# Zero rows under the 33-row halves of the node products of a two-network graph kernel

## The chip, the cores and the metric

The kernel runs on one core of a Trainium2 chip. The metric is the device time of one execution in microseconds (us), as the median of the runs. A core has a tensor engine (PE in the profile; its weight loads are listed apart as PEld), a vector engine (DVE), a scalar engine (ACT), GpSimd (POOL), which here issues the gathers, and SyncE (SP), which issues most other transfers.

## The reference, cut to what matters

There are 3125 nodes with 128 features and 100000 edges. Two message-passing rounds on 160 features per node come first, then three attention rounds on 128 features. A round of the first network is this, with D = 160:

```python
ecat = jnp.concatenate([h[src], h[dst]], axis=-1)
em = jax.nn.relu(_layernorm(ecat @ wm.T + bm, gm, bem)) * w[:, None]
msum = jax.ops.segment_sum(em, dst, num_segments=n)
messages = msum / (cnt + 1e-08) * valid
tw = jax.nn.sigmoid(h @ wg.T + bg)
h_new = jax.nn.relu(_layernorm(jnp.concatenate([h, messages], axis=-1) @ wu.T + bu, gu, beu))
return tw * h_new + (1 - tw) * h
```

After the two rounds the result is multiplied by `w_out`, each row is normalised and added to the input, and the attention rounds start from that. The node products, `h @ wm.T` (in two halves, one for the source and one for the target of an edge), the two halves of the product with `wu.T`, and `h @ w_out.T`, have 160 rows to sum over. The array of PE takes 128, so each is made of two matmuls that add up in PSUM: one over features 0 to 127, and one over features 128 to 159 with a row of ones for the bias, 33 rows of data.

## The kernel before

**Tiling.** Nodes stand in 28 blocks of 112 rows, edges in 812 tiles of 128, sorted by target. A round has a node part and an edge part. In the edge part (the loop around lines 1203, 1224 and 1227) POOL gathers one row of a node table per edge, one indirect transfer per tile (line 557), at most 32 tiles ahead of PE. PE adds the target's part with a one-hot matmul (line 1224) to the gathered rows (line 1227), ACT and DVE normalise, and PE sums the messages by target with a second one-hot matmul (line 1203), which DVE adds to the accumulator (line 1792).

**The node part between two edge parts.** All of it is in four quarters of seven blocks. `updated(q)` on PE turns seven blocks of summed messages (two transposes each, lines 1236 and 1237), ACT copies them from PSUM to `MT1` and `MT2` (lines 931 and 932), and PE multiplies them with `WU1` (line 1248, 128 rows) and `WU2` (line 1249, 33 rows). DVE's `update(q)` takes the seven results out of PSUM (line 1620), normalises them with a square root made by ACT (line 854) and ends with the quarter's new features (line 1640, milestone `h{l}_{q}`). `products(q)` on PE waits for that milestone, turns the seven new blocks (lines 1126 and 1128, copies by ACT at lines 846 and 848 to `HT1` and `HT2`) and multiplies them with `WPQ1` (line 1266, 128 rows) and `WPQ2` (line 1267, 33 rows); ACT copies the results out (line 964). The program order of PE is `updated(0)`, `updated(1)`, `products(0)`, `updated(2)`, `products(1)`, `updated(3)`, `products(2)`, `products(3)`. ACT makes the roots of quarter q+1 in the middle of `products(q)`, behind its fourth block's copies.

**After the quarters.** At the end of round 0 the table goes to memory and POOL may begin the gathers of round 1. PE goes on with the target's half of the next round's product, 28 more blocks (`taq1`, lines 1171 and 1172, taken out by DVE at line 1666), and only then starts the edge part of round 1. At the end of round 1 the product with `w_out` takes the place of the table, DVE also normalises the rows (`rows_out`), and the attention rounds follow. At the very start, `tab0` and `taq0` (the same lines 1171 and 1172, 56 blocks) stand beside POOL's scatter of the sorted edges (line 542). In both edge parts, 28 blocks are also multiplied with the first half of `WU1` and `WU2` inside the loop (lines 1210 and 1211).

**Where things stand.** Everything lies in one big array `AR` of which `carve(n, parts)` gives out n columns; it moves on by n columns whatever number of partitions is asked. `HT2`, `MT2`, `WPQ2` and `WU2` are carved with 33 partitions, so the 95 partitions below them are never written by that name. Each engine's order is that of its program; a semaphore is awaited where the code says.

Of the kernel before, what the change touches and what calls it, by code (L numbers as in the profile page):

```python
# [14 lines left out]
B = 112  # L15
# [45 lines left out]
D = 160  # L61
# [51 lines left out]
def gnn_program(nc, a, out):  # L113
    with ExitStack() as ctx:
# [41 lines left out]
        STE = carve(4 * 1024).rearrange("p (g n) -> p g n", g=4)  # L156
        sort_end = cur[0]
        HT1 = carve(3 * B).rearrange("p (g n) -> p g n", g=3)
        HT2 = carve(3 * B, 33).rearrange("p (g n) -> p g n", g=3)
        MT1 = carve(3 * B).rearrange("p (g n) -> p g n", g=3)  # L160
        MT2 = carve(3 * B, 33).rearrange("p (g n) -> p g n", g=3)

        gB = carve(D)
        nbeB = carve(D)
# [2 lines left out]
        guB = carve(D, B)  # L167
        beuB = carve(D, B)
        WPQ1 = carve(2 * D)
        WPQ2 = carve(2 * D, 33)  # L170
        BLb = carve(GW, B)
        BRb = carve(GW, B)
        BPQ = BLb[0:1, :]
        WU1 = carve(2 * 161)
        WU2 = carve(2 * 161, 33)
        BU = carve(161, 1)
        attB = gB[:, 0:GW]
        att2B = nbeB[:, 0:128]
# [115 lines left out]
        WP2v = WPQ2.rearrange("p (k f) -> p k f", k=2)  # L294
        WU1v = WU1.rearrange("p (k f) -> p k f", k=2)
        WU2v = WU2.rearrange("p (k f) -> p k f", k=2)
        XJ1 = XJ.rearrange("p (g f) -> p g f", f=D)
        HZ = AR[:, NB * 128:NB * 128 + 16 * 4 * GW]

# [743 lines left out]
        def tensor_program(e):  # L1043
# [110 lines left out]
            for l in range(2):  # L1154
                for p, c0 in ((f"tab{l}", 0), (f"taq{l}", D))[l:]:

                    for b in range(-1, NB):
                        if b + 1 < NB:
                            w.wait_ge(s_dve, DV["henc"] if l == 0 else DV["h0_3"])
                            turn_block(p, b + 1, H, (b + 1) % 2, True)  # L1160
                        if b < 0:
                            continue
                        o = PS[2 + b % 4][0:B, 0:D]
                        w.wait_ge(s_ts, tp_at(p, b))
                        w.wait_ge(s_dve, DV[f"w{l}"])
                        if p == "tab0":
                            w.wait_ge(s_aev, aev_at(p, b - 4))
                        else:
                            w.wait_ge(s_aev, aev_at(f"tab{l}", NB - 1))
                            w.wait_ge(s_dev, dev_at(p, b - 4))  # L1170
                        e.matmul(o, HT1[:, b % 3, :], WPQ1[:, c0:c0 + D], start=True, stop=False)
                        done(e.matmul(o, HT2[:, b % 3, :], WPQ2[:, c0:c0 + D], start=False, stop=True), s_mm)

                w.wait_ge(s_dve, DV[f"wf{l}"])
                w.wait_ge(s_dev, dev_at(f"taq{l}", NB - 1))
# [4 lines left out]
                for j in range(-2, NQ + 2):  # L1180
# [14 lines left out]
                    for u in (2 * j, 2 * j + 1):  # L1195
                        v_ = u - 4
                        if 0 <= v_:

                            w.wait_ge(s_vt, pair_at(l, v_))
                            w.wait_ge(s_sw, quad_at(l, v_ // 2))  # L1200
                            w.wait_ge(s_acc, pair_at(l, v_ - 2) if v_ >= 2 else 0)
                            for t in (2 * v_, 2 * v_ + 1):
                                x = e.matmul(PS[4 + v_ % 2][0:B, (t % 2) * 161:(t % 2 + 1) * 161], SW[:, (t // 4) % 4, t % 4, :],  # L1203
                                             VB[:, v_ % 6, t % 2, :], start=True, stop=True, skip_group_check=True)
                            b = OWN[l].get(v_ // 2 - 1) if v_ % 2 == 0 else None
                            if b is not None:

                                o = PS[4][0:B, 322:483]
                                w.wait_ge(s_tsu, own_at(l, b))
                                e.matmul(o, HT1[:, b % 3, :], WU1v[:, 0, :], start=True, stop=False, skip_group_check=True)  # L1210
                                x = e.matmul(o, HT2[:, b % 3, :], WU2v[:, 0, :], start=False, stop=True, skip_group_check=True)
                            done(x, s_scat)
                        if 0 <= u < 2 * NQ:
                            if l == 0:
# [24 lines left out]
                def updated(q, bank):  # L1239
                    for k in range(-1, CH):  # L1240
                        b = q * CH + k
                        if k + 1 < CH:
                            sums_turned(b + 1)
                        if k < 0:
                            continue
                        o = PS[bank + BANK[k]][0:B, PLACE[k] * 161:(PLACE[k] + 1) * 161]
                        w.wait_ge(s_tsu, upd_at(l, b))
                        e.matmul(o, MT1[:, b % 3, :], WU1v[:, 1, :], start=True, stop=False, skip_group_check=True)
                        done(e.matmul(o, MT2[:, b % 3, :], WU2v[:, 1, :], start=False, stop=True, skip_group_check=True), s_mmu)

                def products(q, bank):
                    p, n = ("tab1", D) if l == 0 else ("out", 128)
                    w.wait_ge(s_dve, DV[f"h{l}_{q}"])
                    for k in range(-1, CH):
# [9 lines left out]
                        else:  # L1264
                            w.wait_ge(s_w[5], 48)
                        e.matmul(o, HT1[:, b % 3, :], WPQ1[:, 0:n], start=True, stop=False, skip_group_check=True)
                        done(e.matmul(o, HT2[:, b % 3, :], WPQ2[:, 0:n], start=False, stop=True, skip_group_check=True), s_mm)


                p = "tab1" if l == 0 else "out"  # L1270
# [112 lines left out]
        def vector_program(e):  # L1383
# [6 lines left out]
            def mile(inst, name):  # L1390
                _, n = w.done(inst, s_dve)
                assert n == DV[name], (n, name)
# [148 lines left out]
            for i in range(2):  # L1541
                x = e.tensor_copy(BT[:, i * (T // 2):(i + 1) * (T // 2)], PS[6 + i][0:1, 0:T // 2])
            mile(x, "bt")
            mile(e.memset(HT2[32:33, :, :], 1.0), "ht1")

            w.wait_own()
# [547 lines left out]
```

## Time and profile before

| | |
|---|---|
| median of 3 runs | 7023.26 us (7016.12 to 7036.81) |
| profiled execution, its own time | 7019.37 us |
| its span on the core | 7017.6 us |
| PE, PEld, DVE, ACT, POOL busy | 77%, 65%, 63%, 36%, 66% |
| chain that ended last, by engine | PE 17%, POOL 16%, DVE 15%, issue 10%, DMA 4% |
| costliest groups | gathers of the attention rounds (line 565) 2304.1 us, gathers of the two first rounds (line 557) 1543.6 us |

The page gives shares of the whole span. The stages have different limits, so it is read together with the views by time: the busy times and the granted clock of PE in a stretch, the engines' instructions in order of time, and the chain of waits. Times in those views count from the start of the span. One float32 matmul shows as two records of the same line ("x2"), and a transpose as one; ends of matmuls are modelled, so the spacing of starts is what is measured.

### The profile page before, as it was taken

Reading aid. Unit: us, or ns where it says so; the run is one execution under the profiler, and the core shown is the slowest. Engines: PE = TensorE matmul, PEld = TensorE weight load, DVE = VectorE, ACT = ScalarE, POOL = GpSimd, SP = SyncE. Lnnn points to the kernel's source line nnn. Section 1 sums busy time; section 2 is a strip of 40 time slices with the busy share of each in tenths; the row PEclk is TensorE's granted clock in tenths of the full one; section 3 lists DMA queues with packets and bytes.
Section 4 is the critical chain, followed back from the end, with each engine's and each line's share of the span. In section 5 each row is a group of like instructions: output and inputs, shape, how many; then the busy total and the mean of one; then the engine's idle time right before and its main releaser. Section 6 shows DMA issues by size and latency. Waiting matters only on the chain.

```text
span 7017.6 us, 115824 instructions
## 1 busy us (share of the span) xinstructions
PE 5415.8 (77%) x33441; PEld 4579.1 (65%) x33441; DVE 4449.0 (63%) x15289; ACT 2517.0 (36%) x9692; POOL 4645.8 (66%) x4865
## 2 busy tenths in 40 slices
PE   7998871888888888788867777767777776777776
PEld 6655550777776587777656666666666665666665
DVE  5434320777776488877656776765777774767775
ACT  2554420777776378777511111110111111111112
POOL 1777776777775277777337777727777754777771
PEclk9999999999998589999769999978999997999996
DMA  3111111444444155555324444434444453444442
GB/s 105 42 40 36 41 23 61 130 125 129 125 129 90 53 153 152 153 141 143 60 80 138 135 137 131 135 78 128 134 138 138 130 120 87 135 138 135 139 126 41
DMA packets 397380, 764.25 MB, mean 109 GB/s; under 512 B 111024, under 2 KB 256293, under 8 KB 395993
## 3 DMA queue, kind: packets, MB, share of 16 engines
q0 software_dynamic: 180928, 315.57, 20.9%
q1 hardware_dynamic: 211482, 426.96, 18.3%
q10 hardware_dynamic: 4352, 14.30, 0.7%
q8 instruction: 288, 4.72, 0.3%
q14 instruction: 330, 2.70, 0.1%
HBM read 649.40 MB, written 106.24 MB: 108 GB/s over the span
## 4 chain that ended last, share of the span: by engine, by line
PE 17%; POOL 16%; DVE 15%; issue 10%; DMA 4%; DVEq 2%; ACT 1%; SPq 0%; POOLq 0%; ACTq 0%
POOL AR L565 12%; PE PS L1313 5%; DVE AR L1886 4%; POOL AR L557 4%; PE PS L1329 4%; PE PS L1326 3%; DMA AR<-gtab_d,AR 3%; DVE AR L1955 2%; PE PS L1203 1%; PE PS L1227 1%; DVEq L491 1%; DVE AR L1966 1%; PE PS L1224 1%; DMA AR<-ptab_d,AR 1%; DVE AR L1792 1%
## 5 line engine op out<-in xcount | busy, mean ns | idle before, releaser
L565 POOL DMA_INDIRECT AR<-gtab_d,AR x2436 | 2304.1, 946 | 1149.3 <-issue 707.7
L557 POOL DMA_INDIRECT AR<-ptab_d,AR x1624 | 1543.6, 951 | 685.6 <-issue 470.7
L1329 PE MATMUL PS<-AR,ident 128*128 128x140 f32 x4872 | 1110.5, 312 | 250.0 <-DMA AR<-gtab_d,AR 248.6
L1313 PE MATMUL PS<-AR 128*112 128x132 f32 x4872 | 888.3, 316 | 403.7 <-DVE AR L1886 377.1
L1326 PE MATMUL PS<-AR 128*128 x4872 | 1092.2, 309 | 83.8 <-issue 83.7
L1313 PEld LDWEIGHTS PS<-AR 128*112 128x112 f32 x4872 | 698.0, 199 | 549.0 <-DVE AR L1886 257.4
L1329 PEld LDWEIGHTS PS<-AR,ident 128*128 128x128 f32 x4872 | 842.8, 211 | 315.5 <-DMA AR<-gtab_d,AR 313.4
L542 POOL DMA_INDIRECT rec_d<-AR x782 | 789.1, 1009 | 388.0 <-issue 235.1
L1966 DVE SCALAR_TENSOR_TENSOR AR<-PS,AR 128x280 f32<-128x280 f32 x1218 | 537.3, 445 | 697.8 <-PE PS L1329 695.3
L1010 ACT ACTIVATE AR<-AR 128x448 f32<-128x448 bf16 x609 | 334.9, 570 | 1788.3 <-PE PS L1313 1583.4
L1227 PE MATMUL PS<-AR,ident 128*128 128x160 f32 x3248 | 774.9, 321 | 213.6 <-DMA AR<-ptab_d,AR 210.5
L1886 DVE TENSOR_TENSOR AR<-AR,PS 112x132 f32 x2436 | 697.2, 286 | 341.1 <-PE PS L1313 119.4
L1326 PEld LDWEIGHTS PS<-AR 128*128 128x128 f32 x4872 | 837.7, 211 | 109.2 <-issue 107.7
L1792 DVE TENSOR_TENSOR AR<-AR,PS 112x161 f32 x1624 | 519.6, 320 | 416.3 <-PE PS L1203 162.5
L1224 PE MATMUL PS<-AR 112*128 x3248 | 748.4, 312 | 13.3 <-issue 12.1
L1227 PEld LDWEIGHTS PS<-AR,ident 128*128 128x128 f32 x3248 | 544.0, 198 | 292.1 <-DMA AR<-ptab_d,AR 286.5
L1203 PE MATMUL PS<-AR 128*112 128x161 f32 x3248 | 608.2, 311 | 98.6 <-DVE AR L1792 89.1
L923 ACT ACTIVATE AR<-PS 128x160 f32<-128x160 f32 x1624 | 492.4, 303 | 389.0 <-PE PS L1227 293.9
L1224 PEld LDWEIGHTS PS<-AR 112*128 112x128 f32 x3248 | 552.6, 198 | 39.4 <-issue 39.3
L1801 DVE SCALAR_TENSOR_TENSOR AR<-PS,AR 128x160 f32<-128x160 f32 x1624 | 549.4, 380 | 28.9
L1203 PEld LDWEIGHTS PS<-AR 128*112 128x112 f32 x3248 | 487.9, 184 | 114.0 <-issue 106.0
L895 ACT ACTIVATE AR<-AR 128x112 f32<-128x112 f32 x1624 | 491.3, 374 | 11.7 <-DVE AR L1717 11.7
(335 smaller groups left out, 7735.3 us busy)
## 6 DMA issues: line engine op xcount, KB each, us to landing
AR<-ste_d SPq DMA_DIRECT2D x404, 512.0 KB
AR<-nbb_d SPq DMA_DIRECT2D x303, 224.0 KB
ste_d<-AR SPq DMA_DIRECT2D x101, 512.0 KB
AR<-gtab_d,AR POOLq DMA_INDIRECT x2436
AR<-ptab_d,AR POOLq DMA_INDIRECT x1624
nbb_d<-AR SPq DMA_DIRECT2D x101, 224.0 KB, 2.1
AR<-key_d SPq DMA_DIRECT2D x94, 224.0 KB
rec_d<-AR POOLq DMA_INDIRECT x782, 2.1
```

The costliest lines, as they stand in the source:

```text
L542: e.indirect_dma_start(out=rec_d[:, :], out_offset=bass.IndirectOffsetOnAxis(ap=rowi[:, n:n + 1], axis=0), in_=REC[:, c * RW:(c + 1) * RW] ...
L557: e.indirect_dma_start(out=XJ1[:, t % 32, :], out_offset=None, in_=tabs_d[0][:, :], in_offset=off).then_inc(done_, 16)
L565: e.indirect_dma_start(out=xj2(t)[:, t % 4, :], out_offset=None, in_=tabs_d[1][:, :], in_offset=off).then_inc(done_, 16)
L1203: x = e.matmul(PS[4 + v_ % 2][0:B, (t % 2) * 161:(t % 2 + 1) * 161], SW[:, (t // 4) % 4, t % 4, :], VB[:, v_ % 6, t % 2, :], start=True, s ...
L1224: e.matmul(o, STE[0:B, ste_slot(l, t), (t % 8) * 128:(t % 8 + 1) * 128], TABQ[0:B, bass.ds(block_of(cp, "tensor", t), 1), :], start=True, ...
L1227: x = e.matmul(o, ident[:, :], XJ1[:, t % 32, :], start=False, stop=True, skip_group_check=True)
L1313: x = e.matmul(PS[6 + v_ % 2][0:B, (t % 2) * 132:(t % 2 + 1) * 132], SQ4[:, i % 4, t % 4, :], PX[:, i % 5, t % 4, :, :].rearrange("p h c - ...
L1326: e.matmul(o, STE[:, ste_slot(l + 2, t), (t % 8) * 128:(t % 8 + 1) * 128], TABG[:, bass.ds(block_of(cp, "tensor", t), 1), :], start=True, ...
L1329: x = e.matmul(o, ident[:, :], xj2(t)[:, t % 4, :], start=False, stop=True, skip_group_check=True)
L1792: x = e.tensor_tensor(o, o, PS[4 + v_ % 2][0:B, (t % 2) * 161:(t % 2 + 1) * 161].unsqueeze(1), ALU.add)
L1886: x = e.tensor_tensor(o, o, PS[6 + v_ % 2][0:B, (t % 2) * 132:(t % 2 + 1) * 132].rearrange("p (a h c) -> p a h c", a=1, h=4), ALU.add)
L1966: done(e.scalar_tensor_tensor(AB[:, j % 2, kk:kk + 2, :], PS[u % 4][:, 0:2 * GW].rearrange("p (k f) -> p k f", k=2), 0.0, attB.unsqueeze(1 ...
```

## The change

The four 33-row tensors get all 128 partitions (`HT2z`, `MT2z`, `WPQ2z`, `WU2z`), stand side by side as `PADS`, 1314 columns, and DVE zeroes `PADS` once, before the ones row of `HT2` is written. The old names are views of the upper 33 partitions, so all that writes or loads data is as before. The five second matmuls take the 128-row forms. The other carves move within `AR`, and the total stays.

```diff
-        HT2 = carve(3 * B, 33).rearrange("p (g n) -> p g n", g=3)
+
+        PAD0 = cur[0]
+        HT2z = carve(3 * B).rearrange("p (g n) -> p g n", g=3)
+        MT2z = carve(3 * B).rearrange("p (g n) -> p g n", g=3)
+        WPQ2z = carve(2 * D)
+        WU2z = carve(2 * 161)
+        PADS = AR[:, PAD0:cur[0]]
+        HT2, MT2, WPQ2, WU2 = HT2z[0:33, :, :], MT2z[0:33, :, :], WPQ2z[0:33, :], WU2z[0:33, :]
...
+        WU2zv = WU2z.rearrange("p (k f) -> p k f", k=2)
...
-                        done(e.matmul(o, HT2[:, b % 3, :], WPQ2[:, c0:c0 + D], start=False, stop=True), s_mm)
+                        done(e.matmul(o, HT2z[:, b % 3, :], WPQ2z[:, c0:c0 + D], start=False, stop=True), s_mm)
...
-                                x = e.matmul(o, HT2[:, b % 3, :], WU2v[:, 0, :], start=False, stop=True, skip_group_check=True)
+                                x = e.matmul(o, HT2z[:, b % 3, :], WU2zv[:, 0, :], start=False, stop=True, skip_group_check=True)
...
-                        done(e.matmul(o, MT2[:, b % 3, :], WU2v[:, 1, :], start=False, stop=True, skip_group_check=True), s_mmu)
+                        done(e.matmul(o, MT2z[:, b % 3, :], WU2zv[:, 1, :], start=False, stop=True, skip_group_check=True), s_mmu)
...
-                        done(e.matmul(o, HT2[:, b % 3, :], WPQ2[:, 0:n], start=False, stop=True, skip_group_check=True), s_mm)
+                        done(e.matmul(o, HT2z[:, b % 3, :], WPQ2z[:, 0:n], start=False, stop=True, skip_group_check=True), s_mm)
...
+            v(e.memset(PADS, 0.0))
+            w.wait_own()
             mile(e.memset(HT2[32:33, :, :], 1.0), "ht1")
```

On DVE, before the first product, this stood in a row (output shapes, partitions x columns):

```order
L1539 TENSOR_SCALAR AR<-AR 28x812
L1542 CAST AR<-PS 1x406 x2
L1544 MEMSET AR 1x336
L1549 MEMSET AR 2x3136
L1551 MEMSET AR 1x11
```

and this stands there now:

```order
L1544 TENSOR_SCALAR AR<-AR 28x812
L1547 CAST AR<-PS 1x406 x2
L1549 MEMSET AR 128x1314
L1551 MEMSET AR 1x336
L1556 MEMSET AR 2x3136
```

One memset is new, ahead of the ones row for which ACT's first copies wait; the rest keeps its order.

On PE, this is the start of the node part behind round 0, the last messages (line 1203), then transposes and products of the first block:

```order
L1203 MATMUL PS<-AR 112x161 x8
L1236 MATMUL PS<-ident,AR 128x112
L1237 MATMUL PS<-ident,AR 33x112
L1236 MATMUL PS<-ident,AR 128x112
L1237 MATMUL PS<-ident,AR 33x112
L1248 MATMUL PS<-AR 112x161
L1249 MATMUL PS<-AR 112x161
```

and now, with line numbers five higher:

```order
L1208 MATMUL PS<-AR 112x161 x8
L1241 MATMUL PS<-ident,AR 128x112
L1242 MATMUL PS<-ident,AR 33x112
L1241 MATMUL PS<-ident,AR 128x112
L1242 MATMUL PS<-ident,AR 33x112
L1253 MATMUL PS<-AR 112x161
L1254 MATMUL PS<-AR 112x161
```

No instruction of PE moves, and none is added or gone. The output shapes stay too; what differs is the number of rows that the second product reads and loads as weights, 128 for 33, which these rows don't show.

## Rows read from the trace of the kernel before

**Rows 1.** Line 557, POOL's gathers of rounds 0 and 1: min/median/max ns, first and last start.

```profile
L557 POOL DMA_INDIRECT AR<-ptab_d,AR x1624: 940/946/1703, 1213.4 to 3415.5; - x181
```

**Rows 2.** POOL in order of time, start of round 1: start us, us, idle before.

```profile
2379.66 0.94 POOL L557 DMA_INDIRECT AR<-ptab_d,AR  x1 [147.81 <-DMA ptab_d<-AR]
...
2436.12 1.16 POOL L557 DMA_INDIRECT AR<-ptab_d,AR  x1 [16.75 <-PE PS L1227]
```

**Rows 3.** Stretches: us, busy of PE, PEld, DVE, ACT, POOL, PEclk, DMA, GB/s.

```profile
1300.00:2200.00 900.00, 769.39 (x5181) 704.16 (x5180) 638.36 (x2548) 709.47 (x2922) 681.42 (x718) 0.98 0.45 127
...
2254.00:2264.00 10.00, 10.00 (x32) 6.00 (x32) 1.87 (x6) 1.62 (x8) 0.00 (x0) 0.50 0.00 1
...
2400.00:2424.00 24.00, 23.27 (x72) 13.87 (x72) 4.45 (x15) 4.38 (x22) 14.80 (x16) 0.50 0.24 58
...
2460.00:3427.00 967.00, 791.05 (x4950) 730.73 (x4949) 758.14 (x3178) 753.11 (x3038) 724.26 (x763) 0.94 0.54 144
```

**Rows 4.** PE in order of time, one block of `updated(0)` and the next one's start.

```profile
2256.33 0.45 PE L1236 MATMUL PS<-ident,AR 112*128 112x112 f32 x1
2256.58 0.39 PE L1237 MATMUL PS<-ident,AR 112*33 112x112 f32 x1
2256.76 0.74 PE L1248 MATMUL PS<-AR 128*112 128x161 f32 x2
2257.44 0.88 PE L1249 MATMUL PS<-AR 33*112 33x161 f32 x2
2258.24 0.45 PE L1236 MATMUL PS<-ident,AR 112*128 112x112 f32 x1
```

**Rows 5.** PE in order of time, 128-row products of the first attention round.

```profile
3581.62 0.68 PE L1304 MATMUL PS<-AR 128*112 128x140 f32 x2
3582.09 0.67 PE L1303 MATMUL PS<-AR 128*112 128x140 f32 x2
...
3583.27 0.40 PE L1304 MATMUL PS<-AR 128*112 128x140 f32 x2
3583.50 0.40 PE L1303 MATMUL PS<-AR 128*112 128x140 f32 x2
```

**Rows 6.** DVE in order of time, quarter 1 behind round 0, evictions to new features.

```profile
2277.92 2.14 DVE L1620 SCALAR_TENSOR_TENSOR AR<-PS,AR 112x161 f32<-112x161 f32 x7
...
2287.81 0.20 DVE L1409 RECIPROCAL AR<-AR 112x7 f32<-112x7 f32 x1 [5.03 <-ACT AR L854]
...
2296.66 1.33 DVE L1640 TENSOR_TENSOR AR<-AR 112x1120 f32<-112x1120 f32 x1
```

**Rows 7.** ACT in order of time, the square-root table loaded in the same quarter.

```profile
2286.18 1.28 ACT L854 ACT_TABLE_LOAD   x1
```

**Rows 8.** PE in order of time, start of `products(3)`, and of round 1's loop.

```profile
2355.62 0.42 PE L1126 MATMUL PS<-ident,AR 112*128 112x112 f32 x1 [5.19 <-DVE AR L1640]
...
2431.22 0.90 PE L1224 MATMUL PS<-AR 112*128 x2 [2.27 <-issue]
```

**Rows 9.** DVE in order of time, first and last of 28 evictions of `taq1`.

```profile
2372.27 0.32 DVE L1666 COPY AR<-PS 112x160 f32<-112x160 f32 x1 [11.60 <-PE PS L1172]
...
2423.30 0.33 DVE L1666 COPY AR<-PS 112x160 f32<-112x160 f32 x1 [1.28 <-PE PS L1172]
```

**Rows 10.** The chain that ended last behind round 1: start us, us, what.

```profile
3432.97 0.45 PE PS L1236
...
3461.24 0.42 PE PS L1126
...
3472.34 1.34 DVE AR L1630
...
3592.35 8.82 DMA gtab_d<-AR
```

**Rows 11.** DVE in order of time behind the scatter, before round 0.

```profile
1209.92 0.96 DVE L1686 COPY AR<-AR 128x812 f32<-128x812 f32 x1 [140.94 <-DMA AR<-rec_d]
```

**Rows 12.** Line 1544, the memset of the ones row: min/median/max ns, first and last start.

```profile
L1544 DVE MEMSET AR<- x1: 338/338/338, 846.2 to 846.2; 1x336 f32 x1
```

More of the change, by code:

```diff
@@ L158, in gnn_program @@
         HT1 = carve(3 * B).rearrange("p (g n) -> p g n", g=3)
-        HT2 = carve(3 * B, 33).rearrange("p (g n) -> p g n", g=3)
+        PAD0 = cur[0]
[5 more added lines that the diff above has]
+        HT2, MT2, WPQ2, WU2 = HT2z[0:33, :, :], MT2z[0:33, :, :], WPQ2z[0:33, :], WU2z[0:33, :]
         MT1 = carve(3 * B).rearrange("p (g n) -> p g n", g=3)
-        MT2 = carve(3 * B, 33).rearrange("p (g n) -> p g n", g=3)
         gB = carve(D)
@@ L169, in gnn_program @@
         WPQ1 = carve(2 * D)
-        WPQ2 = carve(2 * D, 33)
         BLb = carve(GW, B)
@@ L174, in gnn_program @@
         WU1 = carve(2 * 161)
-        WU2 = carve(2 * 161, 33)
         BU = carve(161, 1)
```

## The prediction, made before the changed kernel was run

> **What bounds the kernel now.** I read the rows by time first, since the page's shares mix stages. In the edge parts of rounds 0 and 1, POOL sets the pace. Its gathers start at 1213.4 us and end at 3415.5 us [rows 1]. From the restart at 2436.12 to that last one, 779 gathers take 979.4 us, 1.257 us each [rows 1, 2], so PE can be faster there and nothing is gained. The exceptions lie between edge parts. POOL's first gather of round 1 follows 147.81 us of idle time, and one of 16.75 us comes after 32 gathers, when PE has not yet begun the loop [rows 2]. The reader should see two things there. What fills those gaps is the node part, where PE is the engine awaited; and PE is busy all the time in it (10.00 of 10 us) while its granted clock is 0.50, the 1.2 GHz level [rows 3]. In the edge parts around it, with less of PE busy, the clock is 0.98 and 0.94 [rows 3], nearly always the 2.4 GHz level.
>
> **The cost of a block now.** In `updated(0)` the starts stand 0.25, 0.18, 0.68 and 0.80 us apart, 1.91 us a block [rows 4]. Compare 128-row products that follow one another: 0.47 us apart at the slow level and 0.23 us at the fast one, for 140 columns [rows 5]. For 161 columns this is 0.54 and 0.27 us. So the 33-row product costs 0.14 us before it (0.68 less 0.54), 0.26 us behind it (0.80 less 0.54), and the transpose after that another 0.06. These are the places where the height changes between 128 and 33 rows, and the next weights are loaded with nothing beside them. Nothing of the kind stands between the transpose with 33 output rows and the 128-row product (0.18 us), or between 128-row products [rows 4, 5].
>
> **What the change does to a block.** All products have 128 rows and all transposes 112. Without the extras a block is two products and two transposes: 2 x 0.54 + 2 x 0.185 = 1.45 us at the slow level, 2 x 0.27 + 2 x 0.09 = 0.73 us at the fast one (the fast transpose is an estimate, half of the slow one). ACT's copies are no new bound: two copies a block, and the next block's transposes are a whole product pair ahead.
>
> **Does the clock rise?** This decides between 1.45 and 0.73. Stretches in which PE is fully occupied with 128-row products do get the fast level: the spacing falls from 0.47 to 0.23 us within one unbroken run [rows 5]. The stretches that stay slow while PE is busy are those with a 33-row product in every block, for the whole of `taq1` too, at 23.27 busy of 24 us [rows 3]. In these only about half of the time has 112 or more rows of data in the array. I take it that low products count little, and that with zeros below them they count in full. So the clock should rise some three blocks into each unbroken run, and fall again where PE waits several us. The Trainium skill speaks against this: TensorE: Matmul & The Clock Gate, Part 1 (The HAM clock gate), lets the clock follow how busy PE has been, and has no rows in it. By that page the busy node part should be fast already; the trace has 0.50, so the measurement decides, and what the page leaves of the matter is the second rival.
>
> **The sum, against the profiled time of 7019.4 us (3.9 us below the median).**
> 1. `updated(0)` behind round 0: 7 x 1.91 = 13.4 us on the path; after, 3 x 1.45 + 4 x 0.73 = 7.3. That is -6.
> 2. From the first quarter's features (2277.9) to the fourth's (2355.5) there are 77.6 us [rows 6, 8]. DVE waits 5.03 us in the first of the three for PE and ACT [rows 6], and more in the later ones. With PE faster, DVE's own chain is next: 9.9 - 5.0 = 4.9 us from its evictions to the sum of squares, about 1.6 us for the root with its table load of 1.28 [rows 7], and 10.2 us to the end of line 1640 [rows 6], 16.7 us a quarter. PE has 14 blocks in that time, 10 us fast and 20 us slow, so it must be fast for two thirds of it. The first quarter begins slow, after PE's wait for line 1640; I give it 18. 18 + 16.8 + 16.8 = 51.6, -26.
> 3. `products(3)`: PE waits 5.19 us for line 1640 first [rows 8] and starts slow: 13.4 to 7.3, -6. The first gather comes 38 us earlier.
> 4. `taq1`: 27 spacings in 51.0 us, 1.89 each [rows 9]. At 0.73 it is 31 us shorter. The loop now starts 51.6 us after the first gather (2431.2 less 2379.7) [rows 2, 8] and would start 20 us after it. POOL may run 32 x 1.25 = 40 us ahead, so its 16.75 us are gone: -16. The rest of the gain in `taq1` is worth nothing, since POOL then sets the end of the round.
> 5. Behind round 1: from the first transpose to the first `products(0)` 28.3 us, with `updated(0)` in it (-6); then 11.1 us to line 1630 of the next quarter [rows 10], of which DVE's own part is about 8.6 (-2.4). The later quarters have `rows_out` on DVE as well and leave PE some 2 us each, twice, and the last 1: -14 in all. The table's write and the attention rounds' gathers come that much earlier, and those rounds are as before.
> 6. The memset: by line 1544's row, 338 ns for 336 columns [rows 12], 1314 columns are 1.3 us; both ends are between 1.1 and 1.4. It delays ACT's first copies. Its cover is POOL's scatter: DVE waits 140.94 us before line 1686 [rows 11], behind all of `tab0` and `taq0`. Cost 0, and 1.3 us without that cover. The blocks of `tab0` and `taq0` get faster under the same cover, for nothing. The 56 blocks multiplied inside the edge parts get faster under POOL's pace, for nothing too.
> Sum: 6 + 26 + 6 + 16 + 14 = 68 us. 7019.4 - 68 = 6951 for a profiled run, 7023.3 - 68 = 6955 for the median. Bounds of this case: if all node parts were fast at once, terms 1, 3 and 5 give another 8 and term 2 another 6 (80 in all, 6941); if the clock comes up one block run later each time, 15 less (6970).
>
> **Rival 1: only the gaps close, the clock stays at 1.2 GHz.** Each block saves 0.46 us. Then 3 (term 1), 13 (term 2, some 28 blocks of PE on the path), 3 (term 3), 12 (term 4: 28 blocks are 13 us, and a stall of some 4 us is left), 10 (term 5): 42 us, 6981. For it: no stretch of the trace has transposes and 128-row products in this mix, and a transpose may count little. Against it: the share of 112- and 128-row work in a slow block rises from about half to nearly all. Chance 0.19.
>
> **Rival 2: nothing changes, 7023.** The gaps might belong to the place and not to the rows, for instance to a second matmul that adds into the same columns. Against it: lines 1224 and 1227 add in the same manner in the loop, at 1.257 us for a whole tile of three matmuls [rows 1, 2], and the only difference at the gap is 33 for 128 rows [rows 4]. The Trainium skill has two statements that would give this result. TensorE: Matmul & The Clock Gate says under LDWEIGHTS (loading the stationary operand) that the load's time goes by columns and that a load of 32 rows takes as long as one of 128, and under Why this matters for your kernels that a single 32-row matmul takes as long as a 128-row one. By these the block would stay at 1.91 us and the sum at 0. The rows agree for the duration of one product and differ for the sequence. Chance 0.07.
>
> **Rival 3: slower.** Round 1's loop begins with POOL some 16 gathers ahead, not 32, so each late gather stops PE sooner. Its idle time lowers the clock in the loop, and PE becomes the bound. Three matmuls a tile are 0.80 us fast and 1.60 us slow; POOL's pace is 1.257. PE falls behind it below a granted clock of about 0.64, and the 68 us are eaten below 0.60. At 0.55 a tile takes 1.45 us: 812 x (1.45 - 1.257) = 157 us, 7112. Against it: round 0's loop had no lead at all and shows 0.98 [rows 3]. Chance 0.04.
>
> **How the numbers follow.** Forecast 0.70, rivals 0.19, 0.07 and 0.04. The likeliest gives 6955. The range goes from its far end, 6940, to just beyond rival 1, 6985. A measurement here tells 0.3% (21 us) from nothing. Faster by more than that: 0.70 + 0.19 = 0.89. Within: 0.07. Slower: 0.04.
>
> **What would show it.** In the node parts, starts of block after block at 1.45 and then 0.73 us, the granted clock at 1.00 for most of `taq1`, no idle time of PEld before the second product's weights. POOL's long wait near 110 us instead of 147.8 and no 16.75 us wait; round 1's gathers in 1020 us from first to last. DVE waiting for ACT's root and hardly for PE. If the blocks stand at 1.45 us throughout, rival 1 holds; at 1.91, rival 2. The forecast is wrong in size if DVE's 16.7 us a quarter is not what is left, or if PE falls slow again in each wait and stays so.

## The result and the profile after

| | before | after |
|---|---|---|
| median | 7019.69 us (7014.18 to 7036.81, 4 runs) | 6936.64 us (6932.25 to 6941.35, 4 runs) |
| profiled execution | 7019.37 us | 6933.67 us |
| its span | 7017.6 us | 6931.7 us |
| ratio, 95% interval | | 0.9878 [0.9858, 0.9897] |

The kernel is 83 us faster, 18 us more than the 6955 that was forecast and 3 us outside the range. The rows below answer to those read before; line numbers are five to seven higher.

PE in order of time, in `updated(0)` behind round 0 (start us, us, engine, line, operation, shapes), which answers to [rows 4]:

```profile
2243.72 0.39 PE L1241 MATMUL PS<-ident,AR 112*128 112x112 f32 x1
2243.91 0.39 PE L1242 MATMUL PS<-ident,AR 112*33 112x112 f32 x1
2244.10 0.75 PE L1253 MATMUL PS<-AR 128*112 128x161 f32 x2
2244.64 0.74 PE L1254 MATMUL PS<-AR 128*112 128x161 f32 x2
2245.17 0.39 PE L1241 MATMUL PS<-ident,AR 112*128 112x112 f32 x1
...
2248.01 0.26 PE L1241 MATMUL PS<-ident,AR 112*128 112x112 f32 x1
2248.11 0.26 PE L1242 MATMUL PS<-ident,AR 112*33 112x112 f32 x1
2248.21 0.44 PE L1253 MATMUL PS<-AR 128*112 128x161 f32 x2
2248.48 0.44 PE L1254 MATMUL PS<-AR 128*112 128x161 f32 x2
2248.76 0.26 PE L1241 MATMUL PS<-ident,AR 112*128 112x112 f32 x1
```

A block takes 1.45 us (2243.72 to 2245.17), and three blocks later 0.75 us (2248.01 to 2248.76), where it was 1.91. The four gaps inside a slow block are 0.19, 0.19, 0.54 and 0.53 us; the two long ones of before, 0.68 and 0.80, are gone.

The granted clock by stretch (us, then busy time and count of PE, PEld, DVE, ACT, POOL, then PEclk, DMA share, GB/s), answering to [rows 3]:

```profile
2240.00:2254.00 14.00, 11.97 (x66) 10.56 (x64) 5.93 (x12) 4.03 (x21) 0.00 (x0) 0.76 0.01 2
2290.00:2303.00 13.00, 10.99 (x81) 10.06 (x82) 12.65 (x17) 6.34 (x35) 0.00 (x0) 1.00 0.01 2
2303.00:2317.00 14.00, 4.90 (x20) 3.78 (x19) 10.10 (x12) 5.35 (x17) 0.00 (x0) 0.61 0.00 0
2325.00:2340.00 15.00, 15.00 (x124) 14.96 (x123) 6.57 (x21) 8.16 (x42) 5.43 (x6) 1.00 0.68 181
```

The clock goes up and down within the node part. It is 1.00 in `taq1`, where PE is busy all the time, and 0.61 where PE waits for DVE. PE has mostly stopped being the engine awaited: in 2303:2317 it is busy for 4.90 of 14 us.

DVE in order of time shows who is late instead (the end of a quarter, line 1647, and its reciprocal, line 1414, which waits for ACT's root), answering to [rows 6]:

```profile
2263.05 1.33 DVE L1647 TENSOR_TENSOR AR<-AR 112x1120 f32<-112x1120 f32 x1
...
2280.93 1.33 DVE L1647 TENSOR_TENSOR AR<-AR 112x1120 f32<-112x1120 f32 x1
...
2288.41 0.20 DVE L1414 RECIPROCAL AR<-AR 112x7 f32<-112x7 f32 x1 [1.26 <-ACT AR L859]
...
2297.25 1.32 DVE L1647 TENSOR_TENSOR AR<-AR 112x1120 f32<-112x1120 f32 x1
...
2313.53 1.33 DVE L1647 TENSOR_TENSOR AR<-AR 112x1120 f32<-112x1120 f32 x1
```

The quarters are 17.9, 16.3 and 16.3 us long, where before they were 20.1, 28.7 and 28.8. In the second of the three DVE waits 1.26 us, for the root; in the first the same wait is 2.81 us. Before, it was 5.03 us in the first and 6.30 in the second.

POOL's waits, after (for what, us in all, times, longest), and its first gather of round 1, answering to [rows 2]:

```profile
POOL AR L570 <- DMA gtab_d<-AR: 393.3, 3, 170.2
POOL AR L562 <- DMA ptab_d<-AR: 110.2, 1, 110.2
POOL AR L562 <- PE PS L1232: 16.8, 55, 0.3
```

```profile
2333.04 0.94 POOL L562 DMA_INDIRECT AR<-ptab_d,AR  x1 [110.20 <-DMA ptab_d<-AR]
```

The wait for the table of round 1 went from 147.8 to 110.2 us. Of the 16.75 us wait nothing is left: the longest wait for PE there is now 0.3 us. The longest wait for an attention table (line 570) was 185.0 and is 170.2.

**The difference by stage.** POOL's transfers divide a span into stages, so I took their starts from each trace: 782 scatters, then five times 812 gathers. Worked out in us:

| stage | before | after | the same kernel again | layout only | 64 rows |
|---|---|---|---|---|---|
| scatter, first to last start | 1026.3 | 1015.8 | 1025.3 | 1025.9 | 1017.7 |
| start of round 0's gathers | 1213.4 | 1203.6 | 1214.1 | 1214.9 | 1205.8 |
| round 0, first to last gather | 1017.5 | 1018.3 | 1017.9 | 1018.7 | 1019.6 |
| last gather of round 0 to first of round 1 | 148.8 | 111.1 | 111.5 | 148.0 | 149.1 |
| round 1, first to last gather | 1035.8 | 1018.3 | 1018.7 | 1036.0 | 1038.6 |
| last gather of round 1 to first attention gather | 186.0 | 171.2 | 175.4 | 186.3 | 186.7 |
| attention rounds, first to last gather | 3267.4 | 3268.3 | 3263.9 | 3267.7 | 3279.0 |
| last gather of all to the end | 148.8 | 140.9 | 152.5 | 144.4 | 144.4 |
| span | 7017.6 | 6931.7 | 6953.9 | 7016.2 | 7023.3 |

The three rows that the change touches give 37.7 + 17.5 + 14.8 = 70 of the 86 us. The rest is 9.8 us before round 0's gathers and 7.9 us behind the last gather, less 1.7 us in the gathers of round 0 and of the attention rounds. (The scatter lies within the row below it; the rows from there on add up to the span.) Neither place holds work that the change makes faster on the path. The last three columns say whether those belong to the change.

### The profile page after: what moved, and what is told of

Its sections match the earlier page's. It is cut to its first block, busy times and chain, and to the rows that moved or that the text cites. A ratio compares the mean times of both kernels' runs of the same rounds, so it can differ in the third digit from the quotient of the medians.

```text
span 6931.7 us, 115825 instructions
## 1 busy us (share of the span) xinstructions
PE 5215.3 (75%) x33441; PEld 4514.8 (65%) x33441; DVE 4454.4 (64%) x15290; ACT 2513.3 (36%) x9692; POOL 4636.7 (67%) x4865
## 4 chain that ended last, share of the span: by engine, by line
POOL 18%; PE 16%; DVE 13%; issue 11%; DMA 5%; DVEq 2%; ACT 1%; POOLq 0%; ACTq 0%
POOL AR L570 10%; POOL AR L562 8%; PE PS L1318 5%; DVE AR L1893 4%; PE PS L1334 4%; PE PS L1331 4%; DMA AR<-gtab_d,AR 3%; DVE AR L1962 2%; DMA AR<-ptab_d,AR 1%; DVEq L496 1%; DVE AR L1973 1%; DVE AR L1983 1%; DVEq L1893 1%; PE PS L1232 1%; PE PS L1208 1%
```

## The experiments

The first four ran on one chip, with a median of before of 7020.28 us (7005.89 to 7042.49, 23 runs). The next four ran on another, with 7012.3 us (7001.04 to 7031.8, 9 runs). The last three are told of apart.

### The changed kernel again

No edit.

> The changed kernel once more. The five terms of the prediction measured 69 us together in its first trace; the rest of the 83 us lay in two places that the change does not touch, POOL's scatter (gathers of round 0 start at 1203.6 us for 1213.4) and the tail behind the last gather (7 to 8 us shorter). Theory A (those are chance of single executions): over more runs the median gain falls towards 70 us (about 6950), and a new trace has the scatter or the tail at another length while the five terms stay at 69 within 3. Theory B (they belong to the change, by the new addresses or by the new phase of everything behind): the gain is 83 again (about 6937) and both places repeat to within 1 us.

6954.08 us (6951.58 to 6956.2, 4 runs), ratio 0.9903 [0.9887, 0.992], a gain of 66 us. In the table above the scatter and the end are back at the length of before (1025.3 and 152.5), and the three rows of the change stay: 37.3, 17.1 and 10.6, in sum 65. So the 16 us beyond the terms are not a fixed part of the change. They are two places where executions differ. In the scatter one transfer in some hundreds takes 12 us in place of 1: a start follows the one before it by more than 8 us twice in 1026.3 us and once in 1015.8 us. At the end, from the last gather's start to the last scatter product of PE, the three traces have 67.9, 59.9 and 71.7 us. From there to the end all three take 80.8 to 80.9 us. What makes either longer was not tried. Of the nine traces with the new places in `AR` on the chips of ordinary speed (two of the changed kernel and one for each of the next seven), seven have the short scatter (1015.0 to 1017.7 us) and two the long one; before has a single trace, a long one, so how often the old layout draws the short one is not known. The next section shows that the layout alone does not gain the 10 us.

### The layout alone

```diff
-                        done(e.matmul(o, MT2z[:, b % 3, :], WU2zv[:, 1, :], start=False, stop=True, skip_group_check=True), s_mmu)
+                        done(e.matmul(o, MT2z[0:33, b % 3, :], WU2zv[0:33, 1, :], start=False, stop=True, skip_group_check=True), s_mmu)
```

and so in all four second products (lines 1177, 1216, 1254 and 1272; the text ahead of the prediction speaks of five, its diff shows these four): the new places in `AR` and the memset are kept, the height of before is back.

> The new carve order and the memset of 1314 columns, with all five second products back at 33 rows. Theory A: nothing, 7020 within 8, blocks at 1.91 us and the clock at 0.50 in the node parts. Theory B (addresses or memset move the scatter and the tail): 10 to 17 us faster, about 7005, with blocks still at 1.91 us. If the memset had a price it would show here alone: up to 1.3 us slower.

7015.75 us (7005.49 to 7032.76, 12 runs), ratio 0.9991 [0.9981, 1.0]. Line 1177, the second product of `tab` and `taq`, has the long loads of before (min/median/max ns):

```profile
L1177 PEld LDWEIGHTS PS<-AR x168: 258/281/308, 959.4 to 2424.7; 33*112 33x112 f32 x168
L1177 PE MATMUL PS<-AR x168: 467/536/607, 959.4 to 2425.0; 33*112 33x160 f32 x168
```

In the changed kernel the medians of this line are 176 and 299 ns. Addresses and memset are worth nothing that stands clear of the noise: the median is 4.5 us lower, the interval reaches 13 us, and the stages that the change shortens are as before in the table (148.0, 1036.0 and 186.3). The rows that the matmul reads are the change.

### 64, 96 and 65 rows

The same four lines with `[0:64, ...]`, `[0:96, ...]` and `[0:65, ...]`.

> All second products over 64 rows for 128. Theory 1 (the gap comes from a change of the array's height, and 33 and 64 rows are the same height): gaps of 0.14, 0.26 and 0.06 us stay, a block is 1.91 us, and since a 64-row product counts for half, the clock stays low: 7020. Theory 2 (the gap comes from a number of rows that is no multiple of 32, or from the rows below being unwritten): the gap goes, 1.45 us a block or less, 6980 or less. Theory 3 (any zeros below raise the clock, though the gap stays): blocks about 1.0 to 1.2 us, about 6960.

> All second products over 96 rows. Theory 1 (heights of 96, 112 and 128 rows go together, as 112 and 128 do): no gaps, 1.45 us a block slow and 0.73 fast, and with three quarters counted for the second product the clock still rises, perhaps a little later: 6940 to 6950, as with 128 rows. Rival (the clock wants all rows): blocks stay at 1.45 us, about 6980 by the terms of the prediction's rival 1. Rival (96 is a height of its own): 7020 or little less.

> All second products over 65 rows, one more than the 64 that kept the gaps. It parts the gap from the clock. Theory 1 (65 rows are of the 128-row height; the clock counts the rows in use): no gaps, so 1.45 us a block slow; with the second product counting for half, the clock rises late or not at all in the node parts, and blocks of 1.45 us are seen over whole stretches: between 6955 and 6985. Theory 2 (the clock does not look at rows, and stayed low only because the gaps left PE without work): no gaps and the clock rises as with 96 and 128 rows: 6940 to 6955, 0.73 us a block for most of the 28 blocks. If the gap stays at 65: 7020.

64 rows: 7023.42 us (7010.51 to 7031.86, 10 runs), ratio 1.0002 [0.9991, 1.0013]. 96 rows: 6945.25 us (6942.26 to 6948.62, 4 runs), 0.989 [0.9874, 0.9907]. 65 rows: 6951.61 us (6940.02 to 6962.22, 4 runs), 0.9906 [0.9885, 0.9927]. PE in order of time with 64 rows:

```profile
2255.20 0.45 PE L1241 MATMUL PS<-ident,AR 112*128 112x112 f32 x1
...
2255.63 0.74 PE L1253 MATMUL PS<-AR 128*112 128x161 f32 x2
2256.30 0.88 PE L1254 MATMUL PS<-AR 64*112 64x161 f32 x2
2257.11 0.88 PE L1253 MATMUL PS<-AR 128*112 128x161 f32 x2
```

and with 65 rows, a few blocks into the stretch:

```profile
2250.65 0.44 PE L1253 MATMUL PS<-AR 128*112 128x161 f32 x2
2250.93 0.44 PE L1254 MATMUL PS<-AR 65*112 65x161 f32 x2
2251.31 0.53 PE L1253 MATMUL PS<-AR 128*112 128x161 f32 x2
```

One row makes the difference. With 64 the gaps of 0.67 and 0.81 us around the second product stand as before, and the clock stays down (0.53 and 0.50 in the two stretches below, the second with PE busy for 30.00 of 30 us). With 65 both are gone, and blocks stand 1.45 us apart at the slow level and 0.74 at the fast one. The number of rows with something in them is nearly the same, so what counts is on which side of 64 the height lies, not how much of the array is filled. The kernel with 65 rows gained the least of those without gaps, 61 us: in its one trace the clock came up later in some runs of blocks (four slow spacings at the start of `updated(3)`), the three quarters take 55.9 us where 96 rows have 52.7 and three traces with 128 rows 50.5 to 52.6, and the first gather of round 1 comes 116.0 us behind the last one of round 0. Whether that is the 65 rows or chance was not repeated; the intervals of the ratios overlap.

```profile
2245.00:2257.00 12.00, 11.65 (x38) 7.16 (x38) 1.65 (x5) 2.73 (x14) 0.00 (x0) 0.53 0.01 2
2370.00:2400.00 30.00, 30.00 (x97) 18.14 (x96) 5.21 (x16) 6.16 (x32) 19.32 (x21) 0.50 0.52 149
```

With 96 rows the second product of a fast block is as with 128 (0.44 us, the next transpose 0.28 us behind its start), and the clock in the stretch of `updated(0)` is 1.00:

```profile
2244.00:2256.00 12.00, 8.82 (x65) 7.83 (x64) 5.99 (x13) 4.92 (x22) 0.00 (x0) 1.00 0.01 3
```

### Ones in place of zeros under the node features

```diff
+            v(e.memset(AR[32:64, PAD0:PAD0 + 6 * B], 1.0))
+            v(e.memset(AR[64:128, PAD0:PAD0 + 6 * B], 1.0))
```

`HT2z` and `MT2z` then have ones below, and the weights' halves keep their zeros, so the sums are the same.

> The changed kernel with ones for zeros in rows 64 to 127, and rows 33 to 63, of the stationary second parts; the moving operands stay zero there, so the products are the same. If the clock goes by the rows that are used and not by their values, blocks are at 0.73 us and the wait between rounds 0 and 1 is 111 us, 6940 to 6955. If values mattered, the clock would rise earlier than with zeros, the wait under 110 us. The two more memsets of 672 columns lie under the scatter: 0.

6939.65 us (two runs, 6935.62 and 6943.67), ratio 0.9891 [0.9868, 0.9914]; line 1177 is at 298/299/474 ns. What the rows of the node features, the operand that is loaded as weights, hold makes no difference. The other operand kept its zeros in every run.

### Only the node products at 128 rows

`updated(q)` and `products(q)` as in the change; `tab`, `taq` and the products in the loop back at 33 rows (lines 1177 and 1215 with `[0:33, ...]`), and the same for their weights.

> 128 rows only for the products of the quarters (updated and products); tab, taq and those inside the edge parts at 33 rows. By the prediction's terms 1, 2, 3 and 5: POOL's wait between rounds 0 and 1 is 111 us as in the changed kernel, and the one behind round 1 some 11 to 15 us shorter. taq1 takes 28 x 1.91 = 53 us again, so the loop starts 61 us after the first gather, later than 32 gathers last (40 us): POOL stalls some 20 us, more than the 16.75 before. Gain 37 + 13 less 3 or so: 6970 to 6978. If taq1's speed were worth nothing, it would be 6954.

6941.88 us (6941.52 to 6942.1, 4 runs), ratio 0.9894 [0.9877, 0.9912]: some 30 us faster than I expected, and as fast as the kernel with all four at 128 rows and ones below. POOL's stages say why: 112.3 us to the first gather of round 1 and 1019.0 us for its gathers, so the 16.75 us wait has not come back. Here is `taq1` of this kernel, the same instructions with 33 rows that stood 1.90 us apart before:

```profile
2326.60 0.52 PE L1177 MATMUL PS<-AR 33*112 33x160 f32 x2
2327.05 0.32 PE L1131 MATMUL PS<-ident,AR 112*128 112x112 f32 x1
2327.21 0.26 PE L1133 MATMUL PS<-ident,AR 112*32 112x112 f32 x1
2327.30 0.44 PE L1176 MATMUL PS<-AR 128*112 128x160 f32 x2
2327.67 0.52 PE L1177 MATMUL PS<-AR 33*112 33x160 f32 x2
```

and its stretch:

```profile
2325.00:2354.00 29.00, 28.92 (x162) 18.93 (x162) 8.59 (x27) 10.68 (x55) 15.12 (x16) 1.00 0.62 182
```

A block takes 1.07 us at a granted clock of 1.00. In the same execution `taq0`, which no fast block precedes, takes 1.90 us a block (transposes at 1000.03 and 1001.93 us). So **blocks with a 33-row product do not bring the clock up, but while PE goes on without a wait they can hold it**. Before, `taq1` was slow because the stretch ahead of it was slow. The gap at the change of height is there at both levels: 1.07 less 0.74 is 0.33 us at the fast one, 1.91 less 1.45 is 0.46 us at the slow one. I had not thought of this, and the next section puts it to the test.

### One group of products at a time

Three kernels, each with one group at 128 rows and the others at 33: `products(q)`, `updated(q)`, `tab` and `taq`.

> Only the product with WPQ2 in products(q) reads 128 rows; the second products of taq, of updated(q) and of the loop read 33 rows of the new layout. Theory H (a block with a 33-row product cannot lift the clock from 1.2 to 2.4 GHz, but holds it at 2.4 when it comes after a fast block, at 1.07 us a block, as taq1 did in the kernel with only the node products at 128 rows): updated(0) stays at 1.91 us a block behind both rounds; products(q) starts slow and rises after three blocks (7.3 us for seven), updated(q+1) behind it holds the fast level (7.5 us), so a quarter is DVE's 16.7 us as in the changed kernel; taq1 comes behind a fast products(3), holds too, and POOL's 16.8 us wait is gone. Against before: 26 + 6 (products(3)) + 16 + about 8 behind round 1 = 56 us, so 6956 to 6964. Rival R (the level goes by the rows of each block, and the fast taq1 of that kernel was only what was left of the run before it): updated(q+1) falls back to 1.91, a quarter takes 7.3 + 13.4 = 20.7 us, taq1 is slow and POOL's wait returns: 15 + 6 + 5 = 26 us, about 6988.

> Only the product with WU2 in updated(q) reads 128 rows; products(q), taq and the loop read 33. Theory H: updated(0) rises after three blocks as in the changed kernel (6 us each time). products(q) comes behind PE's wait for DVE, at 1.2 GHz, and cannot lift the clock: 13.4 us for seven, then updated(q+1) 7.3: 20.7 us a quarter for 25.9 before, 15 us. products(3) and taq1 stay slow, POOL's 16.8 us wait is about as before. Behind round 1 about 10. In sum 31 us, 6981 to 6990. Rival R gives the same here; a kernel as fast as the changed one (6945) would say that the rows of products(q) do not matter, and one at 7015 that the clock does not rise in updated(q) either.

> Only the products of tab and taq read 128 rows; updated(q), products(q) and the loop read 33. Both theories: the quarters are as before (POOL waits 148 us for the table), taq1 starts slow, rises after about three blocks and takes 3 x 1.45 + 25 x 0.74 = 23 us in place of 53, so POOL's wait of 16.8 us after 32 gathers is gone and round 1's gathers take 1019 us from first to last in place of 1036. Nothing changes behind round 1. 17 us, 6995 to 7003. If the clock does not rise at the end of slow 33-row blocks, taq1 takes 41 us, a wait of some 4 us is left, and the gain is 13.

These ran on a third chip, where transfers were slower: before took 8785.66 us there (8750.52 to 8814.05, 16 runs), and in the three traces round 0's gathers take 1295 to 1321 us from first to last in place of 1018. The times are 8737.26 us (0.9946 [0.9925, 0.9967]), 8757.79 us (0.9975 [0.9957, 0.9993]) and 8722.75 us (0.9938 [0.9919, 0.9957]). The forecasts in us are for another chip, and the order of the three is not the one forecast: the gains are 48, 28 and 63 us, where `taq` alone was to gain least. The traces show why. On this chip `tab0` and `taq0` begin only when the scatter has ended (first product at 1508.7, 1515.4 and 1514.4 us, last scatter at 1424.6, 1431.1 and 1430.4), so nothing covers them. At 128 rows they take 44.5 us from first to last product in place of 105.1, and the first gather comes 147 us behind the last scatter where the other two kernels have 200 and 201. That is 53 us for blocks that were worth nothing on the other chips. So the totals don't answer the question that was asked, and the rest is read from the traces.

The durations of PE are those of the other chips. Worked out from the starts of each block's first product, in us between blocks (a pause in the middle of `products` is the wait for ACT's roots):

| | `updated(2)` | `products(1)` | `taq1` |
|---|---|---|---|
| before | 2.04 1.91 1.91 1.91 ... | 2.04 1.90 1.90 1.90 (pause) 1.61 | 2.04 1.90 1.91 1.90 ... |
| after | 1.58 1.22 0.75 0.74 ... | 0.83 0.74 0.74 0.74 (pause) 0.64 | 0.83 0.74 0.74 ... |
| only `products` | 2.05 1.91 1.90 1.91 ... | 1.57 1.10 0.74 0.74 (pause) 0.64 | 1.16 1.07 for 13 blocks, then 1.90 |
| only `updated` | 1.58 1.44 0.80 0.74 ... | 1.16 1.07 1.07 1.06 (pause) 0.91 | 2.03 1.90 1.90 ... |
| only `taq` | 2.04 1.91 1.90 1.91 ... | 2.04 1.90 1.90 1.90 (pause) 1.60 | 1.58 1.10 0.74 0.74 ... |

Every group of the table at 128 rows that starts slow comes up to 0.74 us within three blocks. Every group of the table at 33 rows goes on at the level at which it is entered: 1.16 and 1.07 behind fast blocks, 2.04 and 1.90 behind a wait. `updated(0)`, which the table leaves out, shows that this is no full rule. It is entered at the fast level, behind waits of 0.72, 1.19 and 0.30 us, and with 33 rows loses it after the first block and stays down, here with only `products` at 128 rows:

```profile
2966.10 0.53 PE L1253 MATMUL PS<-AR 128*112 128x161 f32 x2 [0.30 <-ACT AR L937]
...
2967.26 0.62 PE L1253 MATMUL PS<-AR 128*112 128x161 f32 x2
...
2969.05 0.74 PE L1253 MATMUL PS<-AR 128*112 128x161 f32 x2
```

The first block takes 1.16 us, the second 1.79, the third 1.90, as all that follow. In the kernel before, the level is lost at the same place, within the first block. With 128 rows it was kept there in some traces (only `updated`, 96 rows) and lost in others (65 rows, and the changed kernel run again), and then it came back. So 33-row blocks are not needed to lose it there; whether they add to it is open. Behind a longer wait it is also lost, as in the middle of `products(1)` of the same kernel:

```profile
3027.76 0.53 PE L1271 MATMUL PS<-AR 128*112 128x160 f32 x2 [3.00 <-ACT AR L853]
3028.12 0.43 PE L1272 MATMUL PS<-AR 128*112 128x160 f32 x2
3028.40 0.43 PE L1271 MATMUL PS<-AR 128*112 128x160 f32 x2
3028.67 0.57 PE L1272 MATMUL PS<-AR 128*112 128x160 f32 x2
3029.03 0.39 PE L1241 MATMUL PS<-ident,AR 112*128 112x112 f32 x1
...
3032.15 0.75 PE L1253 MATMUL PS<-AR 128*112 128x161 f32 x2
3032.83 0.87 PE L1254 MATMUL PS<-AR 33*112 33x161 f32 x2
```

After 3.00 us of idle time PE is fast for three more products, and from the fourth on it is slow (transposes 0.39 us long), and `updated(3)` behind it never recovers. In the same kernel `taq1` holds 1.07 us for 13 blocks, in which this stretch has 1.00:

```profile
3071.00:3085.00 14.00, 14.00 (x80) 9.14 (x79) 3.90 (x12) 4.79 (x24) 4.05 (x5) 1.00 0.70 192
```

Then PE stands still several times (2.66 to 11.09 us, with nothing in the profile that it waits for; this chip's traces have such pauses in all three kernels), and the 33-row blocks behind them stay at 1.90 us. Where only `taq` has 128 rows, the blocks behind the same pauses come up again: 1.57, 1.44, 1.44, 1.36, 0.75.

The three quarters, from the first to the last start of line 1647, took 69.4 us with `products` alone, 59.4 with `updated` alone and 77.6 with `taq` alone, for 77.6 before and 50.5 after. So `updated` is worth 18.2 us, `products` 8.2, and in sum 26.4 they are nearly the whole 27.1. POOL's wait for the table goes the same way: 153.6, 143.0 and 166.8 us. For `updated` alone 62 us were forecast, 3 too many. For `products` alone I had expected DVE's 16.7 us a quarter, since the `updated` behind it would hold the fast level. It holds the level that it finds, and finds the slow one, behind the pause for the root. The quarters are 18.7, 25.3 and 25.4 us, so the rival's 20.7 does not hold either: it had left out the pause of some 3 us and DVE's own part behind the last block.

### The last product's bias with 112 rows

The output stage has a product with one row, a row of ones by the bias, behind each 128-row product. It is put on 112 rows in the same way:

```diff
-                done(e.matmul(o, one_row, BL[:, 0:128], start=False, stop=True), s_mm)
+                done(e.matmul(o, ones[0:B, 0:B], BLb[:, 0:128], start=False, stop=True), s_mm)
```

with `BLb` zeroed before the bias is loaded into its first row; the load of the last weights and the bias waits for that memset.

> The changed kernel, and the same done to the last product, whose bias is a 1-row matmul in each of 28 blocks (112 rows now, ones times the bias row with zeros below). In the tail its starts are 0.70 us apart, two a block, at a clock of 0.50. Without gaps 0.43 us slow, 0.21 fast. The first seven blocks take 9.8 us now and about 5 then; each later quarter goes from 11.0 us to DVE's own 8 or so. Gain 5 + 9 = 12 to 14 us over the changed kernel: about 6940 where e1 gave 6954. Rival (the later quarters are DVE's already): 5 us.

6937.0 us (6929.37 to 6944.24, 5 runs), ratio 0.9887 [0.987, 0.9904]. PE in order of time:

```profile
6886.88 0.64 PE L1385 MATMUL PS<-AR 128*112 128x128 f32 x2
6887.31 0.43 PE L1386 MATMUL PS<-AR,ones 112*112 112x128 f32 x2
6887.57 0.38 PE L1385 MATMUL PS<-AR 128*112 128x128 f32 x2
6887.79 0.38 PE L1386 MATMUL PS<-AR,ones 112*112 112x128 f32 x2
6888.01 0.38 PE L1385 MATMUL PS<-AR 128*112 128x128 f32 x2
```

A pair goes from 1.39 us (in the changed kernel) to 0.44 us (6887.57 to 6888.01) once the clock is up, but the 28 pairs take 34.0 us from first to last in place of 41.8, since PE then waits for those that take its results out and the clock falls between (0.75 in 6900:6916). So 8 us are gained in the trace, not the 12 to 14 expected. The totals, 6937.0 against 6939.65 and 6941.88 of two kernels in the same comparison without this edit, cannot tell it from nothing.

## Why the prediction was right, and where not

**The mechanism** was right in its steps: the gaps belong to the change of height, they close with zeros below, the slow block is 1.45 us and the clock rises after some three blocks, to 0.74 (0.73 forecast). Rival 2 fell with the first block, rival 1 with the fourth. Rival 3 too: round 1's loop has a granted clock of 0.94, as before ([rows 3]). One reading under rival 2 was loose: by [rows 4] the two heights do not take the same time, 0.88 us for the 33-row product and 0.74 for the 128-row one. These ends are modelled, and nothing in the sum hangs on it.

**Terms 1 to 3** were 38 us and measured 37.7. In parts: from the first product of `updated(0)` (2251.3 before, 2242.5 after) to the first quarter's end 25.3 us became 20.5, 5 for the 6 forecast; the quarters 27.1 for 26; behind them 6.0 for 6. **Term 4** was 16 and measured 17.5, and 17.1 in the second trace. The loop's start was as forecast: it comes at 2352.9 us, 19.8 us behind the first gather, where 20 were forecast and 51.6 stood before. **Term 5** was 14 and measured 14.8 and 10.6. **Term 6** was 0 for 1.3 us of memset, which took 1.15 us:

```profile
848.09 1.15 DVE L1549 MEMSET AR<- 128x1314 f32 x1 [0.22 <-issue]
```

**The sum** of 68 us measured 70 and 65 in two traces of the changed kernel, and the second comparison's gain was 66 us. The other kernels without gaps in the quarters gained 61 us (65 rows), 70 (node products alone), 73 (ones below) and 75 (96 rows). **The step that failed is the range.** Its low end, 6940, was built from the unknowns of the change alone: how early the clock rises. (The 80 us given for that case are 68, 8 and 6 and so 82, which is what 6941 goes by; the 42 us of rival 1 are 41.) It put at nothing, without giving a reason, the places that the change leaves alone and that move by themselves: the scatter by 10 us, the end by 8 to 12, and the attention rounds, from 3263.9 to 3279.0 us in the table. It did so though the runs of before spanned 21 us even then (7016.12 to 7036.81). The profiled execution of the changed kernel drew the scatter and the end at the short side, and its first comparison is 18 us below the forecast for that reason, as far as the trace of its profiled execution tells. With 10 us more at each end for that the time would have lain inside. That a group of runs can share such a draw is seen in the four of each: 6932.25 to 6941.35 and 6951.58 to 6956.2 don't overlap, for the same kernel. Why they share it is open.

**One reason was wrong without harm to the sum.** I took it that low products count little for the clock and that it would go by rows of data. The 65 rows come up like 128, and 33-row blocks hold the fast level for 29 us of `taq1` once they have it. Term 4 could have been had from the node products alone. And whether the clock stays down because the gaps are time without work, or because of the change of height itself, no run tells: each kernel that closed the gaps also took away the change of height. The Trainium skill, TensorE: Matmul & The Clock Gate, Part 1 (The HAM clock gate), lets the clock follow how busy PE has been. The rows here show PE busy at 50.00 of 50 us with a granted clock of 0.50 (`taq1` with the layout alone) and at 28.92 of 29 us with 1.00 (`taq1` with the node products at 128 rows), the instructions being the same:

```profile
2375.00:2425.00 50.00, 50.00 (x158) 30.17 (x157) 8.45 (x26) 10.36 (x52) 30.24 (x32) 0.50 0.44 123
```

The busy time of the profile alone does not decide the level; what came before does, and whether a change of height is in each block.

## What to carry to other kernels

Where 128-row products alternate with products of 64 rows or fewer, look at the spacing of starts on both sides of the low one and at the granted clock of that stretch; zeros below, to 65 rows or more, cost one memset if the memory lies idle anyway, and here they closed the gap and let the clock rise. Price it by what PE is awaited for: on the other chips all of the 65 to 70 us came from the node parts between the gathers, and the blocks inside the gather-bound loops and beside the scatter gave nothing; on the third, where the scatter did not cover `tab0` and `taq0`, these were worth 53 us. Before giving a range, cut two traces into stages and see how much the untouched ones differ: that spread belongs in it.

## What the hardware showed that was not expected

- 64 rows behave like 33 and 65 like 128: 1.91 us against 1.45 us a slow block, with the clock down or coming up. Blocks with 65, 96 and 128 rows are equally long at each level (1.45 and 0.74 us). Between zeros and ones below the node features no difference was found.
- The level can be kept by what does not raise it: the same 33-row blocks ran at 1.90 us or at 1.07 us in one execution, by what stood ahead of them. It is not always kept: `updated(0)` with 33 rows lost it after one block, behind short waits. Behind an idle time of 3.00 us the level was lost, a microsecond after the work had begun again.
- A one-row product does the same in the last stage: PE is busy for 38.28 of 42 us (6870 to 6912) at 0.50 there, in the changed kernel, and with 112 rows in its place the clock was 0.76 and 0.75.
- Among the 782 scatters, of 1 us for the most part, single ones take 12 us: one or two of them in each trace on the chips of ordinary speed.
